# A recurrent scan on one core: every matmul pass as two 64-column tiles, the candidate's column term from the edge buffers, biases as weight rows, two loads a step

## The reference, cut to what matters

```python
x = x + _L0_conv_ref(_gn(x), ...)
x = x + _L1_conv_ref(_gn(x), weight_ih, bias_ih, weight_hh, bias_hh)    # the scan
x = x + _L2_conv_ref(_gn(x), ...)
x = x + _L3_conv_ref(_gn(x), ...)

def _cell(prev_col, cur_col, weight_ih, bias_ih, weight_hh, bias_hh):
    pad = jnp.pad(prev_col, ((0, 0), (1, 1), (0, 0)))
    x = jnp.concatenate([pad[:, :-2], pad[:, 1:-1], pad[:, 2:]], axis=-1)
    i_vals = jnp.einsum('bhk,ok->bho', x, weight_ih) + bias_ih
    h_vals = jnp.einsum('bhc,oc->bho', cur_col, weight_hh) + bias_hh
    r_i, z_i, n_i = jnp.split(i_vals, 3, axis=-1)
    r_h, z_h, n_h = jnp.split(h_vals, 3, axis=-1)
    r = jax.nn.sigmoid(r_i + r_h)
    z = jax.nn.sigmoid(z_i + z_h)
    n = jnp.tanh(n_i + r * n_h)
    return n * z + cur_col * (1.0 - z)
```

## Time and profile before

| | us |
|---|---|
| median of 3 runs | 661.55 (659.97 to 664.05) |
| the profiled execution | 663.57 |
| its span in the trace | 661.8 |
| PE busy | 595.9 (90%) |
| DVE busy | 497.6 (75%) |
| ACT busy | 456.2 (69%) |
| POOL busy | 269.6 (41%) |

### The profile page before, as it was taken

One profiled execution on the slowest core, in us unless ns is written; L12 is line 12 of the kernel. 1 busy time (PEld: TensorE's weight loads), 2 busy tenths in 40 slices (PEclk: granted clock), 3 DMA queues, 4 the chain that ended last, 5 costly groups with the idle time before them and its releaser, 6 DMA issues.

```text
span 661.8 us, 19857 instructions
## 1 busy us (share of the span) xinstructions
PE 595.9 (90%) x6860; PEld 478.5 (72%) x6860; DVE 497.6 (75%) x1277; ACT 456.2 (69%) x932; POOL 269.6 (41%) x378
## 2 busy tenths in 40 slices
PE   4689888799999999999999999998878777799996
PEld 2223223478888888888888899997666666799996
DVE  6476685557777777777777768789889889867776
ACT  2345657877777777777777897776748997684442
POOL 6454546135555555554555430104485544202200
PEclk9799898979999999999999999999899998899999
DMA  6800000011111111111111210000316665203314
GB/s 236 316 1 0 1 0 9 0 31 35 36 34 34 35 36 34 34 36 34 35 34 36 62 79 1 1 1 1 129 34 219 201 212 164 96 1 128 128 78 176
DMA packets 31200, 45.63 MB, mean 69 GB/s; under 512 B 7088, under 2 KB 25520, under 8 KB 30272
## 3 DMA queue, kind: packets, MB, share of 16 engines
q1 hardware_dynamic: 30080, 44.98, 21.0%
q10 hardware_dynamic: 672, 0.15, 0.1%
q0 software_dynamic: 416, 0.07, 0.1%
HBM read 28.53 MB, written 8.39 MB: 56 GB/s over the span
## 4 chain that ended last, share of the span: by engine, by line
PE 71%; DVE 16%; issue 5%; ACT 5%; POOL 1%; DVEq 0%; ACTq 0%; POOLq 0%
PE psum L634 16%; PE psum L627 13%; PE psum L595 9%; PE psum L618 8%; DVE work L321 5%; PE psum L707 5%; PE psum L845 5%; PE psum L861 5%; PE psum L723 3%; PE psum L765 3%; ACT work L326 2%; DVE small L1161 2%; PE psum L834 2%; PE psum L691 2%; DVE spec L345 1%
## 5 line engine op out<-in xcount | busy, mean ns | idle before, releaser
L634 PE MATMUL psum<-spec,matrices 128*64 128x128 f32 x1512 | 111.7, 283 | 1.0 <-issue 1.0
L627 PE MATMUL psum<-spec,matrices 128*128 128x128 f32 x756 | 106.4, 277 | 2.3 <-DVE spec L1259 2.3
L486 POOL TENSOR_TENSOR spec<-spec 32x120 f32<-32x120 f32 x126 | 59.8, 474 | 119.0 <-DVE spec L1275 119.0
L595 PE MATMUL psum<-spec,matrices 128*64 128x512 f32 x384 | 94.2, 648 | 15.1 <-ACT spec L886 7.5
L765 PE MATMUL psum<-work 128*32 128x128 f32 x2368 | 77.4, 286 | 24.5 <-ACT work L326 22.2
L627 PEld LDWEIGHTS psum<-spec,matrices 128*128 128x128 f32 x756 | 95.2, 193 | 2.5 <-DVE spec L1259 2.5
L634 PEld LDWEIGHTS psum<-spec,matrices 128*64 128x64 f32 x1512 | 81.0, 138 | 16.5 <-issue 1.5
L765 PEld LDWEIGHTS psum<-work 128*32 128x32 f32 x2368 | 68.3, 115 | 33.4 <-issue 27.3
L595 PEld LDWEIGHTS psum<-spec,matrices 128*64 128x64 f32 x384 | 29.9, 148 | 72.8 <-issue 65.7
L321 DVE TENSOR_TENSOR work<-spec,psum 32x512 f32<-32x512 f32 x108 | 73.5, 680 | 9.1 <-PE psum L765 5.8
L461 POOL TENSOR_SCALAR spec<-image,small 32x960 f32<-32x960 f32 (+1 forms) x48 | 55.5, 1157 | 53.2 <-DVE small L1148 28.7
(11 more groups left out here) (140 smaller groups left out, 982.4 us busy)
## 6 DMA issues: line engine op xcount, KB each, us to landing
work<-w_dram SPq DMA_DIRECT2D x33, 512.0 KB, 3.4
spec<-work SPq DMA_DIRECT2D x252, 32.0 KB, 1.8
image<-x_dram SPq DMA_DIRECT2D x3, 2048.0 KB, 11.6
out_dram<-image SPq DMA_DIRECT2D x3, 2048.0 KB, 6.3
image<-x_dram SPq DMA_DIRECT2D x4, 512.0 KB, 5.9
work<-w_dram SPq DMA_DIRECT2D x1, 2048.0 KB, 7.6
out_dram<-image SPq DMA_DIRECT2D x4, 512.0 KB, 2.9
kept<-const_dram SPq DMA_DIRECT2D x1, 192.0 KB, 5.9
```

Source lines behind the costliest of these rows:

```text
L486: nc.gpsimd.tensor_tensor(lower_edge(h, parity), below(mix[h]), below(keep[h]), ALU.subtract).then_inc(lower_ready[h], 1)
L595: last_mm = mm(psum[o, n % 4, :], cv[:, kx, o], rows_[:, 8 * half:8 * half + 8, kx:kx + W], start=kx == 0, stop=kx == 2)
L627: mm(psum[:, 4 * h + g, 0:HB], sv[:, g, :], state[h], start=True, stop=False)
L634: last = mm(psum[o, 4 * h + g, 0:HB], sv[:, 3 + g, o], e, start=False, stop=True)
```

## The change

- Each of PE's matmuls in the scan is made of two matmuls of 64 output columns. The state's part is split into the two halves of the output.
- The candidate's column term no longer reads `columns`; it reads the edge buffers, whose other rows have weights of zero. It gets a semaphore of its own, `h_sum`, for which DVE waits.
- The order of a half step on PE is r and n from the state, the wait, edges r, column term, edges n, z from the state, edges z.
- The biases become weight rows against the rows of ones. Between the third and the fourth group of the convolution DVE spreads them on diagonals, PE turns them with the identity, and ACT copies them into the weights.
- One pair of DMAs a step brings the input column of both halves, after `z_sum` of both.

The diff, cut to its core:

```diff
@@ -130,7 +130,6 @@
...
         bias_s = sm(6)
-        bias_rz = sm(2)
@@ -151,10 +150,11 @@
...
         def edges_of(h, parity):
-            at_ = (2 * h + parity) * HB
+            at_ = (2 * parity + h) * HB
             return upper_e[:, at_:at_ + HB], lower_e[:, at_:at_ + HB]
...
         gr, gz, gn, pre1, pre2, keep, mix = [[scan_buf() for _ in range(2)] for _ in range(7)]
+        bias_z = spec[:, off:off + 4 * C]
         columns = work[:, 0:B * ROWS]
@@ -197,10 +197,12 @@
...
-        bias_ready = sem("bias_ready")
-        cur_in = [[sem(f"cur_in{h}{parity}") for parity in range(2)] for h in range(2)]
+        bias_spread, bias_turned, bias_written = map(sem, ("bias_spread", "bias_turned", "bias_written"))
+        cur_first = [sem(f"cur_first{h}") for h in range(2)]
+        cur_in = [sem(f"cur_in{parity}") for parity in range(2)]
         state_ready = [sem(f"state_ready{h}") for h in range(2)]
         sedge_ready = [sem(f"sedge_ready{h}") for h in range(2)]
+        h_sum = [sem(f"h_sum{h}") for h in range(2)]
         lower_ready = [sem(f"lower_ready{h}") for h in range(2)]
@@ -385,28 +387,34 @@
...
-            def current(h, w, parity):
-                up, lo = edges_of(h, parity)
-                for to, q in ((up, slice(0, P // 2)), (lo, slice(P // 2, P))):
-                    sp.dma_start(to[q], columns[q, ds(w * (2 * HB) + h * HB, HB)]).then_inc(cur_in[h][parity], 16)
+            SIDES = ((upper_e, slice(0, P // 2)), (lower_e, slice(P // 2, P)))
+            def first_current(h):
+                for e, q in SIDES:
+                    sp.dma_start(e[q, 2 * HB + h * HB:2 * HB + (h + 1) * HB],
+                                 columns[q, 2 * HB + h * HB:2 * HB + (h + 1) * HB]).then_inc(cur_first[h], 16)
+            def current(w, parity):
+                for e, q in SIDES:
+                    sp.dma_start(e[q, parity * 2 * HB:(parity + 1) * 2 * HB],
+                                 columns[q, ds(w * (2 * HB), 2 * HB)]).then_inc(cur_in[parity], 16)
...
             sp.wait_ge(columns_ready, B // 2)
-            current(0, 1, 1)
-            current(0, 2, 0)
+            first_current(0)
             sp.wait_ge(columns_ready, B)
             sp.wait_ge(last_columns, 1)
-            current(1, 1, 1)
-            current(1, 2, 0)
+            first_current(1)
+            current(2, 0)
             with sp.Fori(0, (W - 4) // 2) as i:
...
                         sp.wait_ge(z_sum[h], i * 2 + (k + 1))
-                        current(h, i * 2 + (k + 3), (k + 1) % 2)
+                    current(i * 2 + (k + 3), (k + 1) % 2)
             for h in range(2):
                 sp.wait_ge(z_sum[h], W - 3)
-                current(h, W - 1, 1)
+            current(W - 1, 1)
@@ -606,6 +614,13 @@
...
                 conv_group(j, False, False)
+            pe.wait_ge(const_in, 32)
+            pe.wait_ge(bias_spread, 4)
+            for g in range(4):
+                for row in (C, 2 * C):
+                    last = mm(psum[row:row + C, 5, P * g:P * g + P], bias_z[:, C * g:C * g + C], cm["ident"],
+                              start=True, stop=True)
+            last.then_inc(bias_turned, 1)
             conv_group(NG - 1, False, True)
@@ -613,57 +628,47 @@
...
-            def from_column(h, w):
-                mm(psum[:, 4 * h + 3, 0:HB], sv[:, 6, :], columns[:, ds(w * (2 * HB) + h * HB, HB)],
-                   start=True, stop=True)
-            def banks_free(h, w):
-                pe.wait_ge(reset_done[h], w - 1)
-            def from_state(h, w, parity, nth):
-                pe.wait_ge(state_ready[h], w)
-                for g in (0, 2, 1):
-                    mm(psum[:, 4 * h + g, 0:HB], sv[:, g, :], state[h], start=True, stop=False)
-                pe.wait_ge(cur_in[h][parity], nth * 32)
+            HALVES = [slice(i * (P // 2), (i + 1) * (P // 2)) for i in range(2)]
+            def from_state(h, w, g):
+                if g == 0:
+                    pe.wait_ge(state_ready[h], w)
+                for o in HALVES:
+                    mm(psum[o, 4 * h + g, 0:HB], sv[:, g, o], state[h], start=True, stop=False)
+            def from_edges(h, g, parity, starts=False):
+                for o, e in zip(HALVES, edges_of(h, parity)):
+                    last = mm(psum[o, 4 * h + g, 0:HB], sv[:, 3 + g, o], e, start=starts, stop=True)
+                return last
+            def half_step(h, w, parity, nth):
+                from_state(h, w, 0)
+                from_state(h, w, 2)
+                if nth is None:
+                    pe.wait_ge(cur_first[h], 32)
+                else:
+                    pe.wait_ge(cur_in[parity], nth * 32)
                 pe.wait_ge(sedge_ready[h], w)
                 pe.wait_ge(lower_ready[h], w)
-                for g, s in ((0, r_sum), (2, n_sum), (1, z_sum)):
-                    for i, e in enumerate(edges_of(h, parity)):
-                        o = slice(i * (P // 2), (i + 1) * (P // 2))
-                        last = mm(psum[o, 4 * h + g, 0:HB], sv[:, 3 + g, o], e, start=False, stop=True)
-                    last.then_inc(s[h], 1)
+                from_edges(h, 0, parity).then_inc(r_sum[h], 1)
+                from_edges(h, 3, parity, True).then_inc(h_sum[h], 1)
+                from_edges(h, 2, parity).then_inc(n_sum[h], 1)
+                from_state(h, w, 1)
+                from_edges(h, 1, parity).then_inc(z_sum[h], 1)
             pe.wait_ge(scan_w_in, 16 * 14)
-            pe.wait_ge(columns_ready, B // 2)
+            pe.wait_ge(bias_written, 2)
             pe.wait_ge(conv_added, 2 * B)
-            from_column(0, 1)
-            from_state(0, 1, 1, 1)
-            pe.wait_ge(columns_ready, B)
-            pe.wait_ge(last_columns, 1)
+            half_step(0, 1, 1, None)
             pe.wait_ge(stat1, (NG - 1) * KGN + steps_all(GB - 1) + steps_all(1))
-            from_column(1, 1)
-            from_state(1, 1, 1, 1)
-            banks_free(0, 2)
-            from_column(0, 2)
-            def scan_step(w, parity, nth):
-                from_state(0, w, parity, nth)
-                banks_free(1, w)
-                from_column(1, w)
-                from_state(1, w, parity, nth)
-                banks_free(0, w + 1)
-                from_column(0, w + 1)
+            half_step(1, 1, 1, None)
             with pe.Fori(0, (W - 4) // 4) as i:
                 for k in range(4):
-                    scan_step(i * 4 + (k + 2), k % 2, i * 2 + (1 + (k + 1) // 2))
-            scan_step(W - 2, 0, W // 2 - 1)
-            from_state(0, W - 1, 1, W // 2)
-            banks_free(1, W - 1)
-            from_column(1, W - 1)
-            from_state(1, W - 1, 1, W // 2)
+                    for h in range(2):
+                        half_step(h, i * 4 + (k + 2), k % 2, i * 2 + (k // 2 + 1))
+            for w in (W - 2, W - 1):
+                for h in range(2):
+                    half_step(h, w, w % 2, w // 2)
@@ -923,6 +928,12 @@
...
                 conv_group(j, False, False)
+            act.wait_ge(scan_zeroed, 1)
+            act.wait_ge(bias_turned, 1)
+            sv = scan_m[:, :].rearrange("p (k m) -> p k m", m=P)
+            turned = psum[:, 5, 0:4 * P].rearrange("p (k m) -> p k m", m=P)
+            for row, o in ((C, slice(P // 2, P)), (2 * C, slice(0, P // 2))):
+                a(sv[row:row + C, 3:7, o], turned[row:row + C, :, o], ACT.Copy).then_inc(bias_written, 1)
             conv_group(NG - 1, False, True)
@@ -944,15 +955,13 @@
...
                 act.wait_ge(r_sum[h], w)
-                a(gr[h], psum[:, 4 * h, 0:HB], ACT.Sigmoid, bias=bias_rz[:, 0:1]).then_inc(r_gate[h], 1)
+                a(gr[h], psum[:, 4 * h, 0:HB], ACT.Sigmoid).then_inc(r_gate[h], 1)
                 act.wait_ge(z_sum[h], w)
-                a(gz[h], psum[:, 4 * h + 1, 0:HB], ACT.Sigmoid, bias=bias_rz[:, 1:2]).then_inc(z_gate[h], 1)
+                a(gz[h], psum[:, 4 * h + 1, 0:HB], ACT.Sigmoid).then_inc(z_gate[h], 1)
...
                 act.wait_ge(pre_ready[h], w)
-                a(gn[h], pre2[h], ACT.Tanh, bias=bias_s[:, 2:3]).then_inc(n_gate[h], 1)
-            act.wait_ge(bias_ready, 1)
+                a(gn[h], pre2[h], ACT.Tanh).then_inc(n_gate[h], 1)
@@ -1233,6 +1242,12 @@
...
                 conv_group(j, False, False)
+            dve.wait_ge(small_in, 16 * 8)
+            v.memset(bias_z, 0.0).then_inc(bias_spread, 1)
+            dve.wait_ge(bias_spread, 1)
+            v.tensor_copy(bias_z[:, 0:3 * C:C + 1], bias_s[:, 0:3]).then_inc(bias_spread, 1)
+            v.tensor_copy(bias_z[:, 3:3 + C + 2:C + 1], bias_s[:, 3:5]).then_inc(bias_spread, 1)
+            v.tensor_copy(bias_z[:, 3 * C + 5:3 * C + 6], bias_s[:, 5:6]).then_inc(bias_spread, 1)
             conv_group(NG - 1, False, True)
@@ -1251,18 +1266,16 @@
...
-            dve.wait_ge(small_in, 16 * 8)
-            v.tensor_tensor(bias_rz, bias_s[:, 0:2], bias_s[:, 3:5], ALU.add).then_inc(bias_ready, 1)
             for h in range(2):
...
             def new_state(h, w):
```

(4 more changed lines are left out.)

## The result

The changed kernel takes 680.5 us (median of 4 runs, 679.07 to 681.5) against 662.39 for the kernel before (4 runs, 659.97 to 664.05). The ratio is 1.0269, with a 95% interval of 1.0244 to 1.0294: slower by 18 us. The forecast had the side and the mechanism right, but put the time at 690 with a range that began at 682. The changed execution that was profiled took 679.07 us, with a span of 677.3: 15.5 us above the one of before.

The account below looks back on a forecast made before the run. PE bounds the kernel before; after the change a 2.12 us loop through ACT does. Profiled 663.57 us + 27 (scan) + 0.3 (first half steps) + 0.4 (end) gives 691.5, against the median 689.5, say 690; range 682 to 700.

Parts of the forecast that it names:

- The bound before: Scan before the change: PE bounds at 1.89 us a half step, hiding the 1.68 us loop through ACT.
- What the tiles give: PE in the scan: all 14 passes become pairs, 0.35 us of mode changes goes, PE's demand falls to 1.54 us.
- The loop through ACT: Scan after the change: z_sum, z gate, edge copy, edge matmuls take 2.12 us a half step and bound it.
- the forecast's signs: Changed profile: half step 2.12 us, PE idle about 0.5 before L641, ended by L954, ACT waiting for z_sum, clock 1.00.
- z gate and edge copy, 0.69 us: ACT's part of the 2.12 us loop, read from 202.37 to 203.06 us in the profile before.
- four places read to 0.02 us: Reading error of waits and gaps in the loop: 2.08 to 2.17 us, with the bias part 683 to 697 us.
- The start and the convolution: Before the scan and its first half steps: bias work 0, between -1.7 and +1 us; first half steps 0.3 us more.
- The loads: Input-column DMAs, two of 64 KB a step: 1.8 to 3.6 us, covered by 5.0 us, so they cost nothing.
- PE stays the bound: Rival: scan runs as PE's passes and the 1.57 us state loop allow, -41 us, 621 us; chance 5%.
- The two effects cancel: Rival: ACT loop at 1.85 to 1.95 us, time within 1% of no change; chance 2%.
- The gaps remain: Rival: PE's 0.15 us stops come with each operand change, half step 2.42 us, +64 us, 726; chance 3%.
- The clock rival: Rival: idling PE granted 1.2 GHz, loop 3.2 us, 825 us for the whole scan, 706 for a tenth; chance 6%.

Follow-up runs that it names:

- the copy first: Changed kernel with ACT's edge copy of the other half ahead of the z gate instead of behind it: 635.59 us, 0.9569 of the kernel before.

## Why the prediction was wrong in size and right in kind

*The bound before.* Right. Shorter instructions on ACT and another order on ACT changed nothing in the kernel before (0.9981 and 0.999), and the half step stays 1.89 us.

*What the tiles give.* Right. PE has only 14 pairs of passes left, and with the copy first they fit into a half step of 1.62 us. Full tiles for the state alone bring back 0.36 us a half step (2.41 against 2.05); the sum had 0.34.

*The loop through ACT.* Right as a mechanism, by two cuts: take two pairs of passes out of it and the half step falls by 0.22 us; take it apart, and it falls to 1.62. Most of the forecast's signs are there: PE's loads stand 0.5 us before L641 (its matmuls 0.30 by the profile, where the forecast had 0.53), ACT waits for z_sum, no stop of 0.2 us between state and edge matmuls is left, the clock is 1.00, and PE's share in the scan is 85.5% (205.16 of 240), at the upper end. One is not: the profile names "issue", and not L954, as what ended PE's wait.

*The size of the loop.* Here the prediction failed. The term "z gate and edge copy, 0.69 us" was read from rows of gates with a bias operand, and the change takes that operand away. The text named it, "ACT's and DVE's dropped bias operands: 0.06 us each on DVE, off the loop", and gave ACT's nothing, though the z gate is in the loop. It is worth 0.09 us: gate and copy took 0.60 instead of 0.69 (201.60 to 202.20). The rest of the loop was 0.02 longer than in the sum: 0.10 from the copy's end to PE's first matmul (202.30), where the sum had 0.07, the time to the weight load; and 1.35 from there to the next z gate (203.65) instead of 1.32 + 0.04. So 0.60 + 0.10 + 1.35 = 2.05 instead of 2.12, and with the bias operand given back 0.69 + 0.10 + 1.35 = 2.14, as measured. The half steps grew by 18.55 us instead of 27; these 8.5 us are most of the distance, 9, between the forecast of 689.5 and the median of 680.5. Between the two profiled executions the forecast was 12 us too high (691.3 against 679.07), and 3.7 us of that lie outside the half steps; that the medians come so close to the half steps' share alone is scatter between executions. No gate without a bias stood in the trace of before, so the term should have been bounded from both sides, and a near row allowed it: L943, a copy of 120 elements a partition from SBUF without a bias, took 0.30 us there against 0.37 for a gate of 128. With 0.07 less, and 0 as the other end, the forecast's own range would have been 674 to 697. The Trainium skill has the price itself (ScalarE: Activation LUTs, What ACT_TABLE_LOAD costs): each operand of one value a partition adds about 93 ns to an ACTIVATE over one with immediate values. The runs agree, with 0.09 us at the gates and at the tanh.

*The gap of the range.* It reached from 682 to 700 on "four places read to 0.02 us". That covered how well the rows were read, but not that an instruction in the sum was itself changed.

*The smaller terms.* The end of the scan: 0.21 us for 0.4. The start and the convolution: -1.9 us for 0 to 0.3, of which the bias matmuls' effect on the clock is within the -1.7 to + 1 that was given; 0.85 us lies ahead of any changed line, and the first half steps, from the first edge weights to the second edge matmuls, took 0.1 us less (132.68 to 138.78 against 134.45 to 140.67) and not 0.3 more. After the scan it was 1.4 us less where the forecast had nothing, in lines that the change does not touch. The loads: hidden, as said, and tested. DVE's dropped operand: 0.35 to 0.29 us, off the loop, as said. The normalisation behind ACT's two copies was not covered in full, because PE's stretch ahead of it had become shorter by 1.7 us: PE stood 0.70 us there.

*The rivals.* "PE stays the bound" lost at the point that was named for it: the loop did not fall under 1.90. Where it was made to (copy first), the time was 635.6, not 621: a half step of 1.62 us instead of 1.57, and about 1.68 in the mean with the stops at each turn of DVE's loop. The 1.57 was the loop of one half's state; what bounds there is the loop through both halves that runs over the copy, the z gate behind it and DVE's last three steps, which no rival had. The Trainium skill's rule on the drain (TensorEngine Tiling (Array Packing), Key Properties) agrees with the experiment with full tiles, 0.21 us between starts at each change of shape against 0.11 without; in the changed kernel PE didn't have the path, so the time could not show the gain. "The two effects cancel" asked that gate and copy lose 0.2 us of a "fixed 0.69"; they weren't fixed, but lost 0.09, and the loop ended at 2.05, outside its 1.85 to 1.95. "The gaps remain" is refuted by L637 and L641 following each other at 0.22 us for two passes (202.97, 203.19, 203.41). The clock rival didn't come: the granted clock was 1.00. Its own small case was also added up a little high: 3.2 us instead of 2.12 for a tenth of the scan adds 13 us to 690, which gives 703 and not 706.

## What to carry to other kernels

When an engine is at 100%, ask before unloading it which loop comes next and how long it is after the edit: here the loop through ACT was 1.68 us under 1.89, and the edit that took 0.35 us off PE put 0.44 us of passes into that loop. Ask it again after the repair: with the copy first, the bound is a loop through ACT and DVE that no sum had. In an in-order queue, put the instruction that another engine waits for, and whose own input is there early, ahead of the one whose input comes late: the swap of two ACT instructions was worth nothing before the change and 45 us after it. And every instruction in a sum has to be priced in the form that it has after the edit, operands included.

## What the runs showed of the hardware that was not expected

- A bias operand, one column in SBUF, adds 0.09 us to an ACT activation on 128 x 128 float32, whether it reads PSUM (0.28 to 0.37 us) or SBUF (0.31 to 0.40 us), with zeros in it as well (the experiments with the bias of zeros and without bias operands).
- Each turn of DVE's loop went with 0.3 us of standing at its first instruction: 20 such stops with 21 turns, 7 with 7. In the changed kernel the same stops stand in the trace (19 of 0.3 us from 145 to 370 us) and are covered by the wait for ACT; with the copy first they moved the mean half step from 1.62 to about 1.68 us.
- Eight matmuls of no use in an idle stretch of 2.3 us, with the granted clock at 1.00 (the level of 2.4 GHz) behind them instead of a mean of 0.76 between the two levels, took 1.7 us off the stretch that follows (7.07 to 5.37).
